# A differential-attention layer on Trainium2: one of 36 exponentials per head moved from ScalarE to VectorE and GpSimd

## The reference, cut to what matters

```python
# x: (2, 2048, 256) f32, 16 heads, d = 16; values have 32 columns per head
s1 = einsum('bhqd,bhkd->bhqk', q1, k1) * scale      # and s2 from q2, k2
a1 = softmax(where(causal, s1, -inf)); a2 = softmax(where(causal, s2, -inf))
comb = a1 - lam * a2
out = einsum('bhqk,bhkv->bhqv', comb, v)
normed = (out - mean) * rsqrt(var + eps) * (1 - LAM_INIT)    # per head
x = layernorm(x + merged @ Wo)
h = silu((x @ w1) * s1) * ((x @ w2) * s2)            # 256 -> 1024
h = gelu((h @ h1) * hs1); h = gelu((h @ h2) * hs2)    # 1024 -> 1024, twice
x = layernorm(x + (h @ w3) * s3)                      # ternary weights
```

## Time and profile before

| | |
|---|---|
| median of the runs | 1888.8 us |
| the profiled execution: its time, its span | 1889.36 us, 1887.4 us |
| busy in the span: PE, ACT, DVE, POOL | 98%, 75%, 55%, 12% |
| granted TensorE clock, mean | 0.997 of full speed |
| bytes moved | 146.1 MB, mean 77 GB/s |

### The profile page before, as it was taken

How to read it: one execution, slowest core, us unless ns; L and a number is a source line. 1 busy time by engine, 2 the same in 40 slices (tenths; PEclk the granted TensorE clock), 3 DMA queues, 4 the chain that set the end, 5 groups by cost and what they waited for, 6 DMA issues and landing times.

```text
span 1887.4 us, 30736 instructions
## 1 busy us (share of the span) xinstructions
PE 1850.7 (98%) x12160; PEld 1059.8 (56%) x12160; DVE 1030.9 (55%) x2005; ACT 1409.1 (75%) x1702; POOL 233.2 (12%) x308
## 2 busy tenths in 40 slices
PE   7999999999999999999999999999999999999997
PEld 6774333333333333333333335888888888888886
DVE  5556566556655565556556655454545454636343
ACT  4448999999999999999999997444545454545452
POOL 3001211221121112111211121000000000000000
PEclk9999999999999999999999999999999999999999
DMA  8887256534653476346634621001010000000000
GB/s 261 251 259 181 40 90 118 99 68 87 118 107 63 83 118 111 61 82 118 113 60 81 118 61 43 26 12 34 12 34 12 34 12 34 12 34 23 1 12 14
DMA packets 130192, 146.10 MB, mean 77 GB/s; under 512 B 74276, under 2 KB 100516, under 8 KB 122404
## 3 DMA queue, kind: packets, MB, share of 16 engines
...
...
...
## 4 chain that ended last, share of the span: by engine, by line
PE 91%; DVE 5%; DMA 1%; issue 1%; ACT 1%; ACTq 0%; DVEq 0%; PEldq 0%
PE attn_sums_ps L1061 27%; PE split_hid_ps L1665 25%; PE attn_s_ps L1036 20%; PE split_hid_ps L1649 6%; PE split_y_ps L1682 3%; PE proj_qk_ps L527 3%; PE proj_v_ps L537 2%; PE split_y_ps L1605 2%; PE attn_sums_ps L1069 2%; PE split_turn_ps L1593 1%; DVE attn_raw L1207 1%; DVE attn_raw L1196 1%; DMA proj_wv_low_raw<-in_wv 1%; DVE attn_sums_sb L1191 0%; DMA qk_raw<-proj_copies 0%
## 5 line engine op out<-in xcount | busy, mean ns | idle before, releaser
L1006 ACT ACTIVATE attn_probs<-attn_s_ps 128x1024 f32<-128x1024 f32 x1088 | 1002.9, 1128 | 7.9 <-PE attn_s_ps L1036 7.3
L1061 PE MATMUL attn_sums_ps<-attn_probs,heads_v 128*32 128x512 f32 (+3 forms) x5120 | 587.4, 540 | 0.0
L1036 PEld LDWEIGHTS attn_s_ps<-heads_q,heads_k 50*128 50x128 f32 x2560 | 211.9, 184 | 436.7 <-ACT attn_probs L1006 402.2
L1036 PE MATMUL attn_s_ps<-heads_q,heads_k 50*128 50x512 f32 (+3 forms) x2560 | 449.9, 425 | 1.7 <-ACT attn_probs L1006 1.7
L1759 ACT ACTIVATE split_whole<-split_hid_ps,scales 128x512 f32<-128x512 f32 x128 | 88.3, 690 | 274.5 <-PE split_hid_ps L1665 274.3
L987 POOL TENSOR_SCALAR_AFFINE_SELECT attn_probs<-attn_probs 128x512 f32<-128x512 f32 x256 | 180.4, 716 | 830.0 <-ACT attn_probs L1006 830.0
L1665 PE MATMUL split_hid_ps<-split_hid_b,ffn_r 128*128 128x512 f32 x1024 | 240.8, 392 | 0.0
L1665 PE MATMUL split_hid_ps<-split_hid_a,ffn_r 128*128 128x512 f32 x1024 | 238.1, 391 | 0.0
L1665 PEld LDWEIGHTS split_hid_ps<-split_hid_a,ffn_r 128*128 128x128 f32 x1024 | 190.2, 188 | 41.0 <-DVE split_hid_a L1934 0.3
L1665 PEld LDWEIGHTS split_hid_ps<-split_hid_b,ffn_r 128*128 128x128 f32 x1024 | 189.8, 188 | 38.2
L1061 PEld LDWEIGHTS attn_sums_ps<-attn_probs,heads_v 128*32 128x32 f32 x5120 | 107.6, 108 | 174.5 <-issue 139.9
...
## 6 DMA issues: line engine op xcount, KB each, us to landing
...
```

Of the source, the lines that this page charges most:

```text
L1006: nc.scalar.activation(weights, side_by_side, ACT.Exp, scale=SCALE).then_inc(exp_done, 1)
L1036: last = nc.tensor.matmul(s_ps[(NU * h + n) % SLOTS][:, s, col:col + width], k_sb[u][rows, b * SEQ + j * PARTS:b * SEQ + (j + 1) * PARTS], ...
L1061: last = nc.tensor.matmul(sums[c * D:(c + 1) * D, off:TILE], v_sb[u][:, b * KEY_BLOCKS + j, :], probs[k % PROBS][:, b, s, place:place + wi ...
```

## The change

- **Soft step.** In heads 0 to 14 step k = 21 (`SOFT`, the first step of the last tile) is not done by ACT. DVE copies its two score units out of PSUM into `ffn_f` (space of the last four weight chunks), scaled (`soft_take`); then 2^x is worked out in f32 by rounding, a polynomial and an exponent made in integer form. DVE does 1280 of the 2048 columns in 24 instructions (three pieces of 8), POOL 768 columns in 28 instructions (two pieces of 14). Each instruction waits for the one before it on the same engine. POOL's stand between its mask of k = 20 and its masks of k = 31. PE weighs k = 21 after k = 34, and the tile's first weighing is then k = 22.
- **Cuts.** The 16 pieces of the next head's stacks are cut in order of query tile, both batches together, instead of batch by batch. PE waits for four pieces at a time. In DVE's program the cuts, the tiles' parts, the soft step and the two roundings are laid out anew (`head_with_soft`).
- **SP.** The stacks of head h+1 are now loaded once all of head h-1 is scored, the values once it is weighed; the store of head h-1 comes after these loads, and the weight halves after that. 22 halves are loaded in heads 0 to 10, the last eight in head 15, where DVE rounds them in four pairs.
- **Projection.** ACT issues the loads of x for tiles 2 to 7 instead of SP. ACT and POOL now have their attention program twice, behind a branch on the flag `exact`, as PE and DVE already had.

```diff
+        def load_x(eng, t):
+
+            eng.dma_start(xt_raw[t % 2][:, :, :].rearrange("p c n -> p (c n)"), xt_in[t]).then_inc(x_loaded[t % 2], 16)
...
+                    if m == 0 and 1 <= t < LAST:
+
+                        act.wait_ge(v_projected, SUBS * t)
+                        load_x(act, t + 1)
...
+SOFT_PASSES = 8
+POOL_PASSES = 14
+KEPT_CHUNKS = CHUNKS - 4
...
+    SOFT = END[2] + 1
+    SOFT_AT = END[3] - 1
+    SOFT_UNITS = [n for n, (k, _) in enumerate(UNITS) if k == SOFT]
...
+        DVE_PIECES = [(0, 1, slice(TILE // 2, TILE)), (1, 0, slice(0, TILE)), (1, 1, slice(0, TILE))]
+        POOL_PIECES = [(0, 0, slice(0, TILE)), (0, 1, slice(0, TILE // 2))]
+        DVE_STEPS = SOFT_PASSES * len(DVE_PIECES)
+        POOL_STEPS = POOL_PASSES * len(POOL_PIECES)
...
+            def store_head(h):
+
+                sp.wait_ge(diff_ready, NT * h + NT)
+                store_rows(h, slice(0, KEY_BLOCKS))
+
             def head(h, u, r, first, last):
-                sp.wait_ge(probs_free, PROBS + NS * h)
                 if last:
+                    sp.wait_ge(probs_free, PROBS + NS * h)
+                    sp.wait_ge(cut_done, TAIL + CUTS * LAST)
...
-                else:
-                    sp.wait_ge(diff_ready, NT * h + NT)
-                    store_rows(h, slice(0, KEY_BLOCKS))
+                        load_half(n)
...
-                if last:
-
-                    sp.wait_ge(diff_ready, NT * h + NT - 1)
-                    store_rows(h, slice(0, LAST_ROWS))
-                else:
-                    sp.wait_ge(diff_ready, NT * h + NT)
-                    store_rows(h, slice(0, KEY_BLOCKS))
+                        load_half(n)
...
+            def soft_pass(h, step):
+
+                piece, n = divmod(step, POOL_PASSES)
+                b, s, cols = POOL_PIECES[piece]
+                width = cols.stop - cols.start
+                value, rounded, power = soft[:, b, s, cols], rounds[0][:, 0:width], powers[0][:, 0:width]
+                if step == 0:
+                    pool.wait_ge(soft_taken, BATCH * h + 1)
+                else:
+                    pool.wait_ge(soft_pool, POOL_STEPS * h + step)
+                if n == 0:
+                    last = pool.tensor_scalar(rounded, value, ROUNDER, None, ALU.add)
...
+                    if k == END[2] and has_soft(h, exact):
+                        for step in range(POOL_STEPS):
+                            soft_pass(h, step)
...
+                    if k == SOFT and has_soft(h, exact):
+                        continue
...
+                if k == SOFT and has_soft(h, exact):
+                    weights = soft
+                    pe.wait_ge(soft_dve, DVE_STEPS * (h + 1))
+                    pe.wait_ge(soft_pool, POOL_STEPS * (h + 1))
...
+                if k == SOFT_AT and has_soft(h, exact):
+                    weigh(h, u, SOFT)
...
+            def soft_take(h):
+
+                for b, n in enumerate(SOFT_UNITS):
+                    dve.wait_ge(scored, NU * h + n + 1)
+                    nc.vector.tensor_scalar(soft[:, b, :, :], s_ps[(NU * h + n) % SLOTS][:, :, :], SCALE * math.log2(math.e), POWER_SHIFT + math.log2(POWER_LEAD),
+                                            ALU.mult, ALU.add).then_inc(soft_taken, 1)
...
+                    if n == 0:
+                        last = nc.vector.tensor_scalar(rounded, value, ROUNDER, None, ALU.add)
+                    elif n == 1:
+                        last = nc.vector.scalar_tensor_tensor(value, rounded, ROUNDER, value, ALU.subtract, ALU.subtract)
+                    elif n == 2:
+                        last = nc.vector.tensor_scalar(rounded.bitcast(I32), rounded, ROUNDER + POWER_BIAS, 2.0 ** 23, ALU.subtract, ALU.mult)
+                    elif n < SOFT_PASSES - 1:
+                        last = nc.vector.scalar_tensor_tensor(power, value if n == 3 else power, POWER[SOFT_PASSES - 1 - n], value, ALU.add, ALU.mult)
+                    else:
+                        last = nc.vector.scalar_tensor_tensor(value, power, POWER[0], rounded, ALU.add, ALU.mult)
+                    last.then_inc(soft_dve, 1)
...
+            def head_with_soft(h):
+
+                u = 1 - h % 2
+                tile(h, 0)
+                square_heads(h)
+                cut_stacks(h + 1, u, range(0, 3))
+                copy_sums(h, 1)
+                cut_stacks(h + 1, u, range(3, 5))
+                take_turned(h, 1)
+                finish_tile(h, 1)
+                cut_stacks(h + 1, u, range(5, 8))
+                soft_take(h)
+                soft_passes(h, range(0, 5))
+                copy_sums(h, 2)
+                soft_passes(h, range(5, 9))
+                take_turned(h, 2)
+                finish_tile(h, 2)
+                soft_passes(h, range(9, DVE_STEPS))
+                cut_stacks(h + 1, u, range(8, 12))
+                copy_sums(h, 3)
+                cut_stacks(h + 1, u, range(12, 14))
+                take_turned(h, 3)
+                finish_tile(h, 3)
+                round_two(h, 0)
+                cut_stacks(h + 1, u, range(14, CUTS))
+                round_two(h, 1)
+
+            for h in range(LAST):
+                if has_soft(h, exact):
+                    head_with_soft(h)
+                else:
+                    head_of_all(h)
```

204 lines of the change are left out of this document (152 added, 52 removed).

## The result

The changed kernel takes 2554.05 us (median of 4 runs, 2550.8 to 2557.3), the kernel before 1889.1 beside it: a ratio of 1.352, 95% interval [1.350, 1.353]. Slower, as forecast, but 219 us above the predicted 2335 and 124 above the top of the range.

The account below looks back on a forecast made before the run. ACT sets the pace, PE barely ahead. Late stores and POOL's passes add 365 us in heads 1 to 11, 53 in 12 to 14, 15 in head 0, 15 in the last: 448, predicted 2335 us, range 2190 to 2430.

Parts of the forecast that it names:

- the SP term: SP's queue: the store behind stacks and values lands at 45.7, delaying DVE, PE's turn and exp(20), to 64.7 from 36.0.
- A: From the previous head's exp(35) end to exp(20) end: forecast 64.7 us in heads 1 to 11, 49.1 in 12 to 14.
- head 0: No store in front, but its third cut needs batch 1's stacks, there at 32.5; exp(35) at 77.7: +15 us.
- the last: Last head: first tile waits for two roundings, six more between early normalisations: +15 us, between 0 and 25.
- The rival without the SP term: Store lands early or other DMA engines take it; only POOL's lateness and two cuts remain: 2005 us, chance 0.07.
- the price of POOL's passes: POOL's soft step: one-tensor passes at 0.634 us like a mask, products at 1.034; 28 passes 19.9 us alone.
- rival with slower passes: POOL's one-tensor passes priced as products: exp(35) 36 us after exp(20), 2410 us; within the first forecast's 0.86.
- B: From the end of exp(20) to the end of exp(35) in a head: forecast 31.2 us.
- the exclusion: POOL and DVE instructions shut each other out of SBUF: exp(35) 31.2 us after exp(20), 25.8 with no exclusion.
- lateness: POOL's masks of 31 done 27.9 us behind exp(20), needed at 22; with no exclusion exp(35) ends at 25.8.
- The ceiling: ACT loses two units, 1.84 us a head, less a bubble of about 1.0: 12 us in all, 24 at most.

Follow-up runs that it names:

- two buffers: Kernel without any soft step, with head differences in one of two buffers in turn, so tile 0 waits for the store of head h-2: 1892.9 us (1.0016).
- the filler: Changed kernel plus extra score-shaped matmuls on PE before tile 1's turn, product unused; three lengths, the longest 165 in heads 1 to 11: 2555.3, 2561.8, 2542.9 us.

## Why the prediction was right and wrong

**Right: the mechanism and the SP term.** The store behind the stacks, DVE's L1353 behind the store, tile 1's copy, the turn and the scores behind it; every time of this chain came within 1.4 us in head 6, and A within 2.2 us over heads 1 to 11 and 12 to 14. On average over heads 1 to 11 the copy is done at 52.5 (forecast 52.6), and the whole 2.2 lies behind it. In whole heads, over before: head 0 +39.1 (forecast 15), heads 1 to 11 +47.2 each (33.2), 12 to 14 +31.4 (17.7), the last +15.1 (15), where tile 0's copy waits for its roundings and is done at 20.9 (19). The prediction's own sum gives 2337, not 2335. The rival without the SP term (2005) fell with the first landing of 19 us. That the order alone, without the soft step, gives 2056 and with two buffers 1893 shows the cause and not only the place.

**Wrong: one term of the sum, the price of POOL's passes.** "A mask of 512 columns takes 0.634 alone; I take this for POOL's passes with one tensor." They take 1.60 (1.98 into int32) and the products 1.43, not 1.034. The 28 passes are 36.0 us in place of 25.4: 10.6 a head, 159 us of the 219 over 15 heads. The prediction's own rival with slower passes (36, 2410) had the direction, but bounded them by the products; the nearest row, a mask, was the wrong relative, and no row bounded the price above. The run without POOL's passes gives B of 26.0, which is the 25.8 that the prediction had without lateness.

**Wrong in size: who pays for the exclusion.** I added 5.5 us to POOL's 19.9 for turns given to DVE. Alone, the passes take 34.5, and DVE's add 1.5. So POOL's own price was 14.6 too low and the exclusion 4.0 too high: two errors that partly cancel, which is luck. Most of the exclusion is paid by DVE, whose passes are not what a head waits for: without them only 11 us go.

**Not foreseen: the clock.** After the stalls of PE before units 14, 27 and 64 the granted clock is 0.5 for some steps. At the turn this is 1.5 to 2.1 us a head by the filler; from the copy to the end of exp(20) it was 14.4 us, and 12.1 in the forecast. Behind the stall before unit 64 the profile shows the slower steps, and exp(35) comes 42.9 behind exp(20), 1.1 more than the passes explain; no run tried this place by itself. Before unit 14 its share was not separated.

**Head 0** was 25 us above its forecast: 11.7 as in the other heads' B, 7.7 of B more than those. Only head 0's gap before unit 64 is 24.5 us, not 16.8, and POOL's group of the first pass has one such idle time, ended by "issue":

```profile
L1079 POOL TENSOR_SCALAR ffn_f<-ffn_f 128x512 f32<-128x512 f32 x15 | 24.1, 1604 | 8.4 <-issue 7.2
```

It could be a load of the passes' program at their first call; no run tried it. Of the 5.4 in A, 2.2 lie behind the copy as elsewhere; batch 1's stacks, which the third cut waits for, were there 35.6 us into the head and not 32.5.
The Trainium skill (GPSIMD Engine Reference, Instruction dispatch) says that the first call of a freshly loaded kernel pays a load of about 6 us; the 7.2 at the first TENSOR_SCALAR is of that size, but nothing in the trace names its cause.

**The ceiling.** The prediction gave the change at best 0.8 to 1.8 us a head. The run without POOL's passes gives B of 26.0 against 26.6: 0.6 of the 1.84 taken from ACT.
